# Selective scan: side jobs of TensorE, ScalarE and VectorE moved by one or two places in a 24-place table

## Chip, cores and metric

One core of one Trainium2 chip. The metric is the device time of one execution in microseconds, the median of several runs. The kernel is one launch with a first phase (normalisation, input projection, 3x3 depthwise convolution), a scan phase and a last phase (layer norm, output projection, and a second layer). The change lies in the scan phase alone.

## Reference

Cut to the scan, with b = 8 images, K = 4 directions, 192 channels d, 16 states n, and L = 4096 positions:

```python
xs = stack(x_flat, x_wh, flip(x_flat), flip(x_wh))          # [b, k, 192, L]
x_dbl = einsum('bkdl,kcd->bkcl', xs, x_proj_w)              # 6 + 16 + 16 rows
dts, Bs, Cs = split(x_dbl)
delta = softplus(einsum('bkrl,kdr->bkdl', dts, dt_proj_w) + dt_proj_b)
A = -exp(A_logs)
# for each position:
h = exp(delta * A) * h + (delta * u) * B
y = sum_n(h * C)
# then y + xs * Dk, the four directions put back in place and added
```

The directions k = 1 and k = 3 read the image column by column (transposed).

## Kernel before

**Tiles.** Positions are cut into chunks of 1024, four to a direction: 8 x 4 x 4 = 128 chunks. A chunk is two steps (even, then odd), one for each half of the 192 channels. A step is 12 units: 4 groups g of 4 states by 3 blocks j of 32 channels, so one unit is a tile of 128 partitions (4 states x 32 channels) by 1024 positions. There are 3072 units. Below, e0 to e11 are the units of the even step and o0 to o11 those of the odd step. The program is written by hand for each engine as a loop over units, with semaphores between them; a job that belongs to "place x" stands in the body of the loop at unit x of that engine.

**A unit.** VectorE does the recurrence of a unit in one scan instruction (L739) of decay E and drive. The drive comes in three kinds: DIRECT (14 of 24 units; TensorE spreads B over partitions into PSUM, L597, and VectorE multiplies it by delta*u, L717), DIAGONAL (6 units: e5, e7, e9, o1, o3, o5; TensorE forms the product itself with 32 small matmuls against diagonal copies of B, L639), and POOLED (4 units: e8, e10, o2, o4; GpSimd multiplies, L905). PSUM holds the drives of two units in turn, so TensorE fills unit n+1 only when the scan of unit n-1 has ended. ScalarE makes the decay (L823) and the carry (L829), GpSimd weighs the state with C (L913), TensorE sums over states (L661).

**Side jobs.** Once a chunk or step, these pass through one PSUM tile called stage, one after another; each waits until the last one has been read out (the table `held`, L471 to L482):

- project: the rows dts, B and C of the next chunk, TensorE L581 in two halves of 512 positions; ScalarE copies dts (L763) and then the rest (L764); VectorE splits off a low part (split, L711), which later jobs wait for.
- delta: the second projection, TensorE L591 on 6 partitions; ScalarE applies softplus (L773), with a table load before it and one after it.
- turn_b: B turned onto partitions, TensorE L610, ScalarE L792; from it 32 diagonal copies a chunk (ScalarE L807, numbers in DIAG_EVEN and DIAG_ODD).
- rep: five spreads of C and B, TensorE L597, ScalarE L786 (crep, the four groups of C) and L780 (brep, B for GpSimd), in the order of the list REPS, in which None is brep.
- turn_dlu: delta*u turned, TensorE L620, ScalarE L798.

Before the change, TensorE projects at e9 and e10, ScalarE copies at e11, VectorE splits behind the scan of e11, and TensorE does delta at o1, turn_b at o5, the first rep (brep) at o6, a second delta at o9, and reps at o10, o11, e0, e1. The body of TensorE's loop is in this order:

```python
fill(un + 1)
sum_y(...)
# then the side job of this place
```

Of the kernel before, what the change touches and what calls it, by code (L numbers as in the profile page):

```python
# [308 lines left out]
def scan_phase(nc, ctx, T, S):  # L309
# [5 lines left out]
    ORDER = ((1, 0, 0, 0, 2, 3, 2, 3, 1, 3, 1, 2), (1, 3, 1, 3, 1, 3, 0, 0, 0, 2, 2, 2))  # L315
    KIND = tuple(tuple(DIAGONAL if g == GDIAG else POOLED if g == GPOOL and x in pooled else DIRECT for x, g in enumerate(row))
                 for row, pooled in zip(ORDER, ((8, 10), (2, 4))))
    REPS = (None, 1, 0, 3, 2)
    DIAG_EVEN, DIAG_ODD = {0: 3, 1: 4, 2: 4, 3: 4}, {6: 3, 7: 3, 8: 3, 9: 3, 10: 2, 11: 3}
    wx = T("wx", [C, NK, 2, C + NR])  # L320
    dtw = T("dtw", [C + NR, NK * ND])
    dtb = T("dtb", [C, NK * 2])
# [38 lines left out]
    NCHUNK = NSTEP // 2  # L361
# [37 lines left out]
    def t_of(k, ci):  # L399
        return TC * (ci if k < 2 else NCH - 1 - ci)  # L400
# [20 lines left out]
    def fills(un):  # L421
        return tally(un, DIRECT, DIAGONAL)
# [18 lines left out]
    def loaded(m):  # L441
        return 64 * (m // 2 + 1)
# [27 lines left out]
    order = [("x", 0), ("dt", 0), ("bt", 0), ("lt", 0), ("dt", 1)] + [("rep", 0, i) for i in range(5)]  # L470
    for n in range(NSTEP):  # L471
        c = n // 2 + 1
        if n % 2 == 0:
            order += [("rep", c - 1, i) for i in range(3, 5) if n] + [("lt", n + 1)]
            order += [("x", c)] if c < NCHUNK else []
        elif c < NCHUNK:
            order += [("dt", n + 1), ("bt", c), ("rep", c, 0), ("lt", n + 1), ("dt", n + 2), ("rep", c, 1), ("rep", c, 2)]
    for job, last in zip(order[1:], order):
        if last[0] == "rep":
            held[job] = (rep_out, rep_index(*last[1:]) + 1)  # L480
# [91 lines left out]
    def tensor(e):  # L572
        def project(c, sub):
            b, k, ci, _ = steps[2 * c]
            t0 = t_of(k, ci) + sub * 512
            if sub == 0:
                if ("x", c) in held:
                    e.wait_ge(*held["x", c])
                e.wait_ge(u_in, 32 * (b + 1))
            for h in range(2):  # L580
                r = e.matmul(stage[0:C + NR, sub * 512:(sub + 1) * 512], wx[:, k, h, :], view(k, h, t0, 512),  # L581
                             start=h == 0, stop=h == 1)
            if sub:
                r.then_inc(x_done)
# [16 lines left out]
        def rep(c, i):  # L601
            e.wait_ge(*held["rep", c, i])
            e.wait_ge(sx_split, c + 1)
            spread(stage, c, 2 * GPOOL if REPS[i] is None else 2 * REPS[i] + 1).then_inc(rep_done)

# [72 lines left out]
        for un in range(NUNIT + 12):  # L678
            n, x = divmod(un, 12)
            c = n // 2 + 1  # L680
            fill(un + 1)
            if un >= 5 and (un - 5) % 3 < 2 and (un - 5) // 3 < NG * NSTEP:
                sum_y((un - 5) // 3, (un - 5) % 3)
            if n == NSTEP:
                continue
            if n % 2 == 0:
                if x < 2 and n:
                    rep(c - 1, x + 3)
                if x == 7:
                    turn_dlu(n + 1, 0)  # L690
                    turn_dlu(n + 1, 1)
                if x in (9, 10) and c < NCHUNK:
                    project(c, x - 9)
            elif c < NCHUNK:
                if x == 1:
                    delta(n + 1)
                if x == 5:
                    turn_b(c)
                if x == 6:
                    rep(c, 0)  # L700
                if x in (7, 8):
                    turn_dlu(n + 1, x - 7)
                if x == 9:
                    delta(n + 2)
                if x in (10, 11):
                    rep(c, x - 9)

    def vector(e):
        def split(c):
            e.wait_ge(sx_copied, c + 1)  # L710
            e.tensor_tensor(sx[64:96, c % 2, :], stage[64:96, :], sx[64:96, c % 2, :], ALU.subtract).then_inc(sx_split)  # L711

        def multiply(un):
            m, j = un // 12, un % 3
            e.wait_ge(fill_done, fills(un) + 1)
            e.wait_ge(dur_in[m % 2], loaded(m))
            e.tensor_tensor(P[un % 2], dur[:, slot(m, j), :], P[un % 2], ALU.mult).then_inc(mul_done)  # L717

        def scan(un):
            b, k, ci, half, m, g, j = place(un)  # L720
            cc = cell(un)
            init = 0.0 if ci == 0 else car[:, cc:cc + 1]
            decay, drive = E[:, fills(un) % NE, :], P[un % 2]
            if kind(un) == POOLED:
                e.wait_ge(pool_mul_done, pooled(un) + 1)
                decay, drive = P[un % 2], dbu[:, pooled(un) % NDB, :]
            elif kind(un) == DIRECT:
                e.wait_ge(mul_done, muls(un) + 1)
            else:
                e.wait_ge(fill_done, fills(un) + 1)  # L730
            e.wait_ge(exp_done, un + 1)
            if un >= NH:
                e.wait_ge(hc_done, un - NH + 1)
            if has_carry(un - NH):
                e.wait_ge(carried, carries(un - NH))
            if ci:
                e.wait_ge(carried, carries(un - 24))
            step = 1 if k < 2 else -1
            e.tensor_tensor_scan(H[:, un % NH, ::step], decay[:, ::step], drive[:, ::step], init,  # L739
                                 ALU.mult, ALU.add).then_inc(scan_done)  # L740

        e.wait_ge(consts_in, NCONST)
        e.tensor_copy(selb[:], selbf).then_inc(ve_set)
        e.tensor_reduce(dsum[:], ds[:], AX.X, ALU.add).then_inc(skip_made)
        e.wait_ge(skip_made, 1)
        for half in range(2):
            e.tensor_scalar(dg[:, half, :], idn[0:C, 0:C], dsum[:, half:half + 1], None, ALU.mult).then_inc(skip_made)
        split(0)
        for un in range(NUNIT):
            n, x = divmod(un, 12)  # L750
            c = n // 2 + 1
            if kind(un) == DIRECT:
                multiply(un)
            scan(un)
            if c < NCHUNK and n % 2 == 0 and x == 11:
                split(c)

    def scalar(e):
        def project(c):
            e.wait_ge(x_done, c + 1)  # L760
            if c >= 2:
                e.wait_ge(fill_done, fills(24 * (c - 1)))
            e.copy(dts, stage[C:C + NR, :])  # L763
            e.copy(sx[:, c % 2, :], stage[0:C, :]).then_inc(sx_copied)  # L764
# [10 lines left out]
        def rep(c, i):  # L775
            e.wait_ge(rep_done, rep_index(c, i) + 1)
            if REPS[i] is None:
                if c:
                    e.wait_ge(pool_mul_done, pooled(24 * c))
                e.copy(brep[:], stage).then_inc(rep_out)  # L780
            else:
                if c:
                    e.wait_ge(hc_done, last_of(2 * c - 1, g=REPS[i]) + 1)
                else:
                    e.wait_ge(ve_set, 1)
                e.copy(crep[:, REPS[i], :], stage).then_inc(rep_out)  # L786

# [65 lines left out]
        for un in range(NUNIT + 12):  # L853
            n, x = divmod(un, 12)
            c = n // 2 + 1
            exp(un + 1)
            if has_carry(un - 1):
                carry(un - 1)
            if x == 4 and n:
                copy_y(n - 1)  # L860
            if n == NSTEP:
                continue
            if n % 2 == 0:
                if x < 3 and n:
                    rep(c - 1, x + 2)
                if x in DIAG_EVEN:
                    diagonal(c - 1, sum(DIAG_ODD.values()) + sum(DIAG_EVEN[i] for i in range(x)), DIAG_EVEN[x])
                if x == 8:
                    turn_dlu(n + 1)
                if x == 11 and c < NCHUNK:  # L870
                    project(c)
            elif c < NCHUNK:
                if x == 2:
                    delta(n + 1)
                if x == 6:
                    turn_b(c)
                if x == 7:
                    rep(c, 0)
                if x == 8:
                    turn_dlu(n + 1)  # L880
                if x == 10:
                    delta(n + 2)
                if x == 11:
                    rep(c, 1)
                if x in DIAG_ODD:
                    diagonal(c, sum(DIAG_ODD[i] for i in range(6, x)), DIAG_ODD[x])

    def pool(e):
# [9 lines left out]
        def multiply(un):  # L898
            m, j = un // 12, un % 3
            p = pooled(un)  # L900
            e.wait_ge(dur_in[m % 2], loaded(m))
            e.wait_ge(rep_out, rep_index(m // 2, REPS.index(None)) + 1)
            if p >= NDB:
# [3 lines left out]
        def weigh(un):  # L907
            b, k, ci, half, m, g, j = place(un)
            e.wait_ge(scan_done, un + 1)
            e.wait_ge(rep_out, rep_index(m // 2, REPS.index(g)) + 1)  # L910
            if un >= NHC:
# [811 lines left out]
```

## Time and profile before

| | |
|---|---|
| median of 3 runs | 12463.16 us (12460.2 to 12470.74) |
| profiled execution, its own time | 12428.21 us |
| its span | 12426.3 us |
| TensorE matmuls busy | 10745.4 us, 86% |
| VectorE busy | 10724.7 us, 86% |
| ScalarE busy | 8061.8 us, 65% |
| GpSimd busy | 9752.4 us, 78% |
| first and last split (L711) | 632.8 and 10405.3 us |

The busy shares are averages over three phases. The scan phase is the middle one, and the last scan instruction of it starts at 10514.42 us. Inside it one must go by which instruction of VectorE starts late, and what released it: a timeline row carries this in brackets, [idle us <- releaser]. Matmul ends are modelled, so the start of the next matmul is the better measure of how long TensorE was taken.

### The profile page before, as it was taken

How to read it: one execution, taken by the hardware profiler on the slowest of the kernel's cores; microseconds unless marked ns; L12 is line 12 of the kernel's file. 1: busy time of each engine (PE TensorE's matmuls, PEld its weight loads, DVE VectorE, ACT ScalarE, POOL GpSimd, SP SyncE). 2: the span in 40 equal slices, each digit the busy share in tenths (PEclk: the TensorE clock that was granted, in tenths of full speed). 3: DMA queues.
4: the chain of work that ended last, by engine and by line, in shares of the span. 5: the costliest groups of instructions: out<-in, count | busy, mean ns of one | idle time of the engine just before them, and what ended most of it. 6: DMA issues, size and time to landing. Idle time of an engine off the chain costs nothing. (4 is left out here: it accounts for less than half of the span.)

```text
span 12426.3 us, 236253 instructions
## 1 busy us (share of the span) xinstructions
PE 10745.4 (86%) x91896; PEld 5926.8 (48%) x91896; DVE 10724.7 (86%) x6806; ACT 8061.8 (65%) x13314; POOL 9752.4 (78%) x4238
## 2 busy tenths in 40 slices
PE   8978888888888888888888888888888887799999
PEld 5644444444444444444444444444444443678778
DVE  7789999999999999999999999999999998555554
ACT  3366777677777776777677767776777775444443
POOL 2178999899999999999999989998999998433330
PEclk9977888788878887888788878887888887799999
DMA  3344554455445554555455545544554454221220
GB/s 107 110 111 113 123 133 114 111 123 133 115 112 129 133 116 112 128 132 116 112 129 132 118 109 128 132 113 114 124 130 113 115 123 116 68 62 47 62 62 11
DMA packets 380191, 1363.70 MB, mean 110 GB/s; under 512 B 55270, under 2 KB 55974, under 8 KB 375756
## 3 DMA queue, kind: packets, MB, share of 16 engines
q1 hardware_dynamic: 379084, 1348.57, 46.0%
q8 instruction: 739, 12.11, 0.4%
q14 instruction: 368, 3.01, 0.1%
HBM read 983.45 MB, written 364.90 MB: 109 GB/s over the span
## 5 line engine op out<-in xcount | busy, mean ns | idle before, releaser
L913 POOL TENSOR_TENSOR HC<-H,crep 128x1024 f32<-128x1024 f32 x3072 | 7213.5, 2371 | 836.0 <-DVE H L739 831.4
L739 DVE TENSOR_TENSOR_SCAN H<-E,car,psum 128x1024 f32<-128x1024 f32 x1920 | 4479.2, 2343 | 232.0 <-PE psum L639 174.1
L823 ACT ACTIVATE E<-dlr,am 128x1024 f32<-128x1024 f32 x2560 | 2917.0, 1142 | 68.0 <-DVE H L739 65.6
L597 PE MATMUL psum<-sx,selb 96*128 96x512 f32 x4864 | 2192.0, 560 | 694.9 <-DVE H L739 419.9
L661 PE MATMUL psum<-HC,sely 128*32 128x512 f32 x12288 | 2519.3, 706 | 5.9 <-POOL HC L913 5.1
L639 PE MATMUL psum<-diag,dluT 128*32 128x128 f32 x49152 | 1933.2, 317 | 681.4 <-DVE H L739 676.0
L717 DVE TENSOR_TENSOR psum<-dur,psum 128x1024 f32<-128x1024 f32 x1792 | 2167.9, 1210 | 179.4 <-PE psum L597 175.2
L639 PEld LDWEIGHTS psum<-diag,dluT 128*32 128x32 f32 x49152 | 1624.4, 128 | 1307.2 <-DVE H L739 1176.5
L597 PEld LDWEIGHTS psum<-sx,selb 96*128 96x128 f32 x4864 | 1016.5, 242 | 2141.1 <-DVE H L739 862.5
L739 DVE TENSOR_TENSOR_SCAN H<-E,psum 128x1024 f32<-128x1024 f32 x640 | 1455.1, 2283 | 89.6 <-PE psum L639 68.7
L807 ACT ACTIVATE diag<-idn,blt 128x128 f32<-128x128 f32 x4096 | 1335.4, 394 | 4.1
L823 ACT ACTIVATE psum<-dlr,am 128x1024 f32<-128x1024 f32 x512 | 572.6, 1118 | 1117.9 <-DVE H L739 1116.4
L905 POOL TENSOR_TENSOR dbu<-dur,brep 128x1024 f32<-128x1024 f32 x512 | 1212.6, 2368 | 0.0
L739 DVE TENSOR_TENSOR_SCAN H<-psum,car,dbu 128x1024 f32<-128x1024 f32 x384 | 892.5, 2324 | 0.0
L661 PEld LDWEIGHTS psum<-HC,sely 128*32 128x32 f32 x12288 | 404.3, 119 | 1000.9 <-issue 936.8
L896 POOL TENSOR_TENSOR dlu<-dlt,u 96x1024 f32<-96x1024 f32 x256 | 673.2, 2630 | 133.3 <-ACT dlt L773 133.3
L581 PE MATMUL psum<-u,wx 96*102 96x512 f32 x1024 | 712.6, 824 | 29.1 <-DMA u<-scr_xa 29.1
L829 ACT COPY car<-H 128x1 f32<-128x1 f32 x2304 | 417.5, 181 | 482.8 <-DVE H L739 475.0
L620 PEld LDWEIGHTS psum<-idn,dlu 96*128 96x128 f32 x4096 | 530.9, 206 | 372.3 <-issue 249.0
L620 PE MATMUL psum<-idn,dlu 96*128 96x96 f32 x4096 | 596.6, 298 | 70.9 <-ACT brep L780 70.2
L591 PE MATMUL psum<-dlt,dtw 6*96 6x512 f32 x1024 | 597.4, 709 | 4.3 <-DVE sx L711 3.4
L1568 POOL TENSOR_TENSOR y<-y,tmp 96x1024 f32<-96x1024 f32 x64 | 195.1, 3114 | 458.0 <-DMA tmp<-scr_yk 458.0
(135 smaller groups left out, 11216.4 us busy)
## 6 DMA issues: line engine op xcount, KB each, us to landing
dur<-scr_dlu SPq DMA_DIRECT2D x1024, 384.0 KB, 6.8
dlr<-scr_dl SPq DMA_DIRECT2D x1024, 384.0 KB, 6.8
scr_dl<-dlt SPq DMA_DIRECT2D x256, 384.0 KB, 3.0
scr_dlu<-dlu SPq DMA_DIRECT2D x256, 384.0 KB, 6.8
scr_yk<-yt SPq DMA_DIRECT2D x256, 384.0 KB, 8.3
yp<-scr_yk SPq DMA_DIRECT2D x128, 384.0 KB, 8.8
scr_xa<-xs SPq DMA_DIRECT2D x64, 384.0 KB, 3.5
scr_sz<-xs SPq DMA_DIRECT2D x64, 384.0 KB, 3.4
```

Of the source, the lines that this page charges most:

```text
L581: r = e.matmul(stage[0:C + NR, sub * 512:(sub + 1) * 512], wx[:, k, h, :], view(k, h, t0, 512), start=h == 0, stop=h == 1)
L597: r = e.matmul(o[:, sub * 512:(sub + 1) * 512], selb[:, which, :], sx[:, c % 2, sub * 512:(sub + 1) * 512], start=True, stop=True)
L620: r = e.matmul(stage[:, sub * 512 + k * C:sub * 512 + (k + 1) * C], dlu[:, t0:t0 + 128], idn[0:C, 0:C], start=True, stop=True)
L639: r = e.matmul(P[un % 2][32 * q:32 * q + 32, i * 128:(i + 1) * 128], dluT[:, m % 2, i, 32 * j:32 * j + 32], diag[:, i, q, :], start=True, ...
L661: r = e.matmul(yps[32 * j:32 * j + 32, cols], sely[:], HC[:, (3 * i + j) % NHC, cols], start=g == 0 and k == 1, stop=g == NG - 1)
L717: e.tensor_tensor(P[un % 2], dur[:, slot(m, j), :], P[un % 2], ALU.mult).then_inc(mul_done)
L739: e.tensor_tensor_scan(H[:, un % NH, ::step], decay[:, ::step], drive[:, ::step], init, ALU.mult, ALU.add).then_inc(scan_done)
L807: e.mul(diag[:, i // 4, i % 4, :], idn[:], blt[:, i:i + 1]).then_inc(diag_made)
L823: e.activation(o, dlr[:, slot(m, j), :], ACT.Exp, scale=am[:, ae:ae + 1]).then_inc(exp_done)
L896: e.tensor_tensor(shaped(dlu[:], k), shaped(dl, k), view(k, half, t_of(k, ci), TC), ALU.mult).then_inc(dlu_made)
L905: e.tensor_tensor(dbu[:, p % NDB, :], dur[:, slot(m, j), :], brep[:], ALU.mult).then_inc(pool_mul_done)
L913: e.tensor_tensor(HC[:, un % NHC, :], H[:, un % NH, :], crep[:, g, :], ALU.mult).then_inc(hc_done)
```

## The change

Nothing is computed differently, and no instruction is added or removed. TensorE's projection goes from e9, e10 to e10, e11; ScalarE's copies from e11 to o0; the split from behind the scan of e11 to behind the scan of o0. turn_b goes from o5 (TensorE) and o6 (ScalarE) to o3 and o4. The reps change their order, so that brep is the last instead of the first, and their places: o6, o11, e0, e1, e2 on TensorE; TensorE has no side job at o10 now, and ScalarE no rep at o11. The diagonal copies are 19 in the odd step and 13 in the even one, instead of 17 and 15.

```diff
-    REPS = (None, 1, 0, 3, 2)
-    DIAG_EVEN, DIAG_ODD = {0: 3, 1: 4, 2: 4, 3: 4}, {6: 3, 7: 3, 8: 3, 9: 3, 10: 2, 11: 3}
+    REPS = (1, 0, 3, 2, None)
+    DIAG_EVEN, DIAG_ODD = {0: 3, 1: 3, 2: 3, 3: 4}, {6: 3, 7: 3, 8: 3, 9: 3, 10: 2, 11: 5}
...
 # tensor
-                if x < 2 and n:
-                    rep(c - 1, x + 3)
+                if x < 3 and n:
+                    rep(c - 1, x + 2)
...
-                if x in (9, 10) and c < NCHUNK:
-                    project(c, x - 9)
+                if x in (10, 11) and c < NCHUNK:
+                    project(c, x - 10)
...
-                if x == 5:
+                if x == 3:
                     turn_b(c)
...
-                if x in (10, 11):
-                    rep(c, x - 9)
+                if x == 11:
+                    rep(c, 1)
...
 # vector
-            if c < NCHUNK and n % 2 == 0 and x == 11:
+            if c < NCHUNK and n % 2 == 1 and x == 0:
                 split(c)
...
 # scalar
-                if x < 3 and n:
-                    rep(c - 1, x + 2)
+                if x < 4 and n:
+                    rep(c - 1, x + 1)
...
-                if x == 11 and c < NCHUNK:
+            elif c < NCHUNK:
+                if x == 0:
                     project(c)
-            elif c < NCHUNK:
...
-                if x == 6:
+                if x == 4:
                     turn_b(c)
...
-                if x == 11:
-                    rep(c, 1)
```

TensorE from e8 to o6 of a chunk, before. L581 is the projection, L591 delta, L610 turn_b, L639 a diagonal fill, L597 a direct fill or a rep, L661 a sum:

```order
L661 MATMUL psum<-HC,sely 32x512 x6
L581 MATMUL psum<-u,wx 102x512 x2
L597 MATMUL psum<-sx,selb 128x512 x2
L581 MATMUL psum<-u,wx 102x512 x2
L597 MATMUL psum<-sx,selb 128x512 x2
L661 MATMUL psum<-HC,sely 32x512 x3
L639 MATMUL psum<-diag,dluT 32x128 x32
L661 MATMUL psum<-HC,sely 32x512 x3
L591 MATMUL psum<-dlt,dtw 96x512 x2
L639 MATMUL psum<-diag,dluT 32x128 x32
L661 MATMUL psum<-HC,sely 32x512 x6
L639 MATMUL psum<-diag,dluT 32x128 x32
```

The same stretch with the change:

```order
L661 MATMUL psum<-HC,sely 32x512 x6
L597 MATMUL psum<-sx,selb 128x512 x2
L581 MATMUL psum<-u,wx 102x512 x2
L597 MATMUL psum<-sx,selb 128x512 x2
L661 MATMUL psum<-HC,sely 32x512 x3
L581 MATMUL psum<-u,wx 102x512 x2
L639 MATMUL psum<-diag,dluT 32x128 x32
L661 MATMUL psum<-HC,sely 32x512 x3
L591 MATMUL psum<-dlt,dtw 96x512 x2
L639 MATMUL psum<-diag,dluT 32x128 x32
L661 MATMUL psum<-HC,sely 32x512 x6
L610 MATMUL psum<-selb,sx 128x4 x8
```

The first fill (that of e11) is now ahead of both halves of the projection, the second half stands behind the fill of o0 and a sum, and turn_b stands ahead of the diagonal fill of o5.

VectorE around the split, before, and then with the change (the listing calls the scan SCALAR_TENSOR_TENSOR):

```order
L739 SCALAR_TENSOR_TENSOR H<-psum,car,dbu 128x1024
L717 TENSOR_TENSOR psum<-dur,psum 128x1024
L739 SCALAR_TENSOR_TENSOR H<-E,car,psum 128x1024
L711 TENSOR_TENSOR sx<-psum,sx 32x1024
L717 TENSOR_TENSOR psum<-dur,psum 128x1024
L739 SCALAR_TENSOR_TENSOR H<-E,car,psum 128x1024 x2
```

```order
L739 SCALAR_TENSOR_TENSOR H<-psum,dbu 128x1024
L717 TENSOR_TENSOR psum<-dur,psum 128x1024
L739 SCALAR_TENSOR_TENSOR H<-E,psum 128x1024
L717 TENSOR_TENSOR psum<-dur,psum 128x1024
L739 SCALAR_TENSOR_TENSOR H<-E,psum 128x1024
L711 TENSOR_TENSOR sx<-psum,sx 32x1024
L739 SCALAR_TENSOR_TENSOR H<-E,psum 128x1024
```

The split has passed one multiply and one scan (those of o0); the scan of o1 now comes right behind it. (The second listing is of a chunk without carries, at the start of a direction, which is why `car` is missing.)

## Rows read from the trace of the kernel before

**Rows 1.** Page, part 1: busy time of each engine.
```profile
PE 10745.4 (86%) x91896; PEld 5926.8 (48%) x91896; DVE 10724.7 (86%) x6806; ACT 8061.8 (65%) x13314; POOL 9752.4 (78%) x4238
```
**Rows 2.** The split's line: durations in ns, first and last start in us.
```profile
L711 DVE TENSOR_TENSOR sx<-psum,sx x128: 1222/1222/1224, 632.8 to 10405.3; 32x1024 fp32r<-32x1024 f32 x128
```
**Rows 3.** Waits, 1500 to 10500 us, 116 chunks: us in total, times, longest.
```profile
DVE H L739 <- PE psum L639: 223.7, 238, 1.6
...
PEld psum L597 <- ACT dlt L773: 214.9, 117, 2.9
...
DVE psum L717 <- PE psum L597: 134.0, 112, 2.4
DVE sx L711 <- ACT sx L764: 113.6, 61, 1.9
```
**Rows 4.** VectorE's timeline, e10 to o5, next direction odd: start, us, idle before.
```profile
4162.16 2.33 DVE L739 TENSOR_TENSOR_SCAN H<-psum,car,dbu 128x1024 f32<-128x1024 f32 x1
4165.63 1.23 DVE L717 TENSOR_TENSOR psum<-dur,psum 128x1024 f32<-128x1024 f32 x1 [1.14 <-PE psum L597]
...
4171.11 1.22 DVE L711 TENSOR_TENSOR sx<-psum,sx 32x1024 fp32r<-32x1024 f32 x1 [1.87 <-ACT sx L764]
...
4173.63 4.58 DVE L739 TENSOR_TENSOR_SCAN H<-E,car,psum 128x1024 f32<-128x1024 f32 x2
...
4181.98 2.35 DVE L739 TENSOR_TENSOR_SCAN H<-E,car,psum 128x1024 f32<-128x1024 f32 x1 [1.52 <-PE psum L639]
...
4186.48 2.32 DVE L739 TENSOR_TENSOR_SCAN H<-E,car,psum 128x1024 f32<-128x1024 f32 x1
```
**Rows 5.** TensorE's timeline in the same chunk, e9 to o6.
```profile
4161.47 3.66 PE L581 MATMUL psum<-u,wx 96*102 96x512 f32 x4
...
4165.43 3.59 PE L581 MATMUL psum<-u,wx 96*102 96x512 f32 x4
...
4172.04 1.03 PE L661 MATMUL psum<-HC,sely 128*32 128x512 f32 x6
4173.01 1.95 PE L591 MATMUL psum<-dlt,dtw 6*96 6x512 f32 x4
4178.27 3.64 PE L639 MATMUL psum<-diag,dluT 128*32 128x128 f32 x64 [3.31 <-DVE H L739]
4181.68 2.55 PE L661 MATMUL psum<-HC,sely 128*32 128x512 f32 x12
4184.38 1.95 PE L639 MATMUL psum<-diag,dluT 128*32 128x128 f32 x64
4186.62 0.73 PE L597 MATMUL psum<-sx,selb 96*128 96x512 f32 x2 [0.29 <-DVE H L739]
...
4189.13 1.05 PE L610 MATMUL psum<-selb,sx 96*128 96x4 f32 x8
```
**Rows 6.** ScalarE's timeline in the same chunk, e11 to o2.
```profile
4169.06 1.00 ACT L763 COPY dlt<-psum 6x1024 f32<-6x1024 f32 x1 [4.34 <-PE psum L581]
...
4180.88 1.28 ACT L823 ACT_TABLE_LOAD   x1
4182.17 1.12 ACT L823 ACTIVATE psum<-dlr,am 128x1024 f32<-128x1024 f32 x1
```
**Rows 7.** Windows of that chunk: PE, PEld, DVE, ACT, POOL busy, PEclk, DMA share, GB/s.
```profile
4173.00:4178.20 5.20, 1.96 (x7) 0.56 (x4) 5.16 (x4) 2.13 (x3) 3.32 (x2) 0.81 0.00 0
4178.20:4181.90 3.70, 3.63 (x67) 3.35 (x70) 2.25 (x2) 3.65 (x5) 3.70 (x3) 0.50 0.06 19
```
**Rows 8.** TensorE's second projection half where the next direction is even.
```profile
5087.13 1.88 PE L581 MATMUL psum<-u,wx 96*102 96x512 f32 x4
```
**Rows 9.** VectorE's split in that chunk.
```profile
5091.42 1.22 DVE L711 TENSOR_TENSOR sx<-psum,sx 32x1024 fp32r<-32x1024 f32 x1
```
**Rows 10.** Timeline of the softplus at o10: TensorE behind it, and VectorE.
```profile
5051.90 2.08 PE L597 MATMUL psum<-sx,selb 96*128 96x512 f32 x4 [2.45 <-ACT dlt L773]
5051.94 1.21 DVE L717 TENSOR_TENSOR psum<-dur,psum 128x1024 f32<-128x1024 f32 x1
```

More of the change, by code:

```diff
@@ L473, in scan_phase @@
         if n % 2 == 0:
-            order += [("rep", c - 1, i) for i in range(3, 5) if n] + [("lt", n + 1)]
+            order += [("rep", c - 1, i) for i in range(2, 5) if n] + [("lt", n + 1)]
             order += [("x", c)] if c < NCHUNK else []
         elif c < NCHUNK:
-            order += [("dt", n + 1), ("bt", c), ("rep", c, 0), ("lt", n + 1), ("dt", n + 2), ("rep", c, 1), ("rep", c, 2)]
+            order += [("dt", n + 1), ("bt", c), ("rep", c, 0), ("lt", n + 1), ("dt", n + 2), ("rep", c, 1)]
     for job, last in zip(order[1:], order):
```

## Prediction

> **What bounds the kernel.** I read the busy shares first: TensorE and VectorE are both at 86%, GpSimd at 78% [rows 1]. These are averages over three phases, so I took the scan phase by itself. The split occurs 128 times, from 632.8 to 10405.3 us [rows 2], which is 9772.5 / 127 = 76.9 us a chunk. VectorE's own work in a chunk is 24 scans of 2.25 us (two back to back take 4.58 us, and overlap their neighbours by 0.09), 14 multiplies of 1.25 us and a split of 1.25 us, 72.8 us in all [rows 4]. So VectorE sets the pace, and some 4 us a chunk are its waits. The waits over 116 chunks say for what: 223.7 us for diagonal fills (1.9 a chunk), 134.0 us for direct fills (1.2 a chunk), and 113.6 us for ScalarE's copy ahead of the split, in only 61 of 116 chunks, so 1.86 us each time it occurs [rows 3]. What the change does to these three is the whole question. TensorE also waits 117 times for the softplus, 214.9 us [rows 3]; that is the wait which the free place at o10 takes away.
>
> **1. Projection from e9, e10 to e10, e11, the split behind o0.** Half of the chunks are followed by a chunk of an odd direction, whose projection reads the image by columns. There a half takes 3.59 to 3.66 us [rows 5]; for an even direction it takes 1.88 us [rows 8], and the split then follows the scan of e11 (5089.05 + 2.35) without a gap [rows 9]. In the slow chunk VectorE stands 1.14 us at the multiply of e11 and 1.87 us at the split [rows 4], 3.01 us in all.
>
> With the change the fill of e11 is ahead of both halves, so the 1.14 us go. The split I walk through in that chunk. The scan of e9 ends at about 4162.25; a direct fill takes 0.6 to 0.7 us, so the first half starts at 4162.9. A half and a fill behind it take 4165.43 - 4161.47 = 3.96 us, so the sum starts at 4166.9; it holds TensorE for 4173.01 - 4172.04 = 0.97 us; the second half starts at 4167.8 [rows 5]. From there to ScalarE's first copy it is 4169.06 - 4165.43 = 3.63 us, and from that to the split 2.05 us [rows 4 to 6]: the split can start at 4173.5. VectorE wants it when the scan of o0 ends. The scan of e11 would end at 4169.24 - 1.14 = 4168.1, multiply and scan of o0 take 3.5 us, so at 4171.6. A stall of 1.9 us is left, of 3.01. The gain is 1.1 us in 64 chunks, **-70 us**. It is not the whole 3 us, because the second half moves behind a fill and a sum as the split moves behind a unit. In the other 64 chunks there was no stall, and with a half of 1.88 us there is none after: 0.
>
> **2. The diagonal fill of o3.** It starts when the scan of o1 ends and takes 3.64 us at 1.2 GHz, against 1.95 us for the same work at 2.4 GHz [rows 5]. VectorE has one scan of 2.25 us to cover it, and stands 1.52 us [rows 4]. The granted clock was 0.81 over the 5.2 us before it, in which TensorE worked 1.96 us, and 0.50 during it [rows 7]. Delta (L591) now waits for the later split, so it moves from just behind the sum to just behind the split, into that pause. It is 1.95 us of work on 6 partitions in the same stretch, and I take it that the clock still falls in most chunks. In the 64 slow chunks the pause between the sum before it and the fill is shorter, since projection and diagonal fill end later: before, from 4173.0 to 4178.3, 5.3 us; now the second half from 4167.8 holds TensorE to 4170.4, the fill to 4172.3, the sum to 4173.3, and the scan of o1 ends at 4173.5 + 1.25 + 2.3 = 4177.1, so 3.8 us. I give half of these fills the higher clock or part of it. ScalarE then sets the limit: its decay for o4 ends at 4183.29 [rows 6], and the scan of o4, which starts at 4184.24, could be 0.9 us earlier and no more. Half of 0.9 or so, 0.5 us x 64 = **-32 us**. The bounds are 0 and 0.9 x 64 = -58.
>
> By the Trainium skill, "ScalarE: Activation LUTs", section "What ACT_TABLE_LOAD costs", a switch of tables is a load of about 1283 ns and a drain of about 1380 ns, 2.66 us together. The load is 1.28 us here too, but the next activation starts 0.01 us behind it [rows 6], so this trace has no such drain. With two drains the decay of o4 would be 2.8 us later than it is, this term would be 0, and the place left free behind the softplus would be worth more than I give it.
>
> **3. Delta itself at the lower clock.** Where the clock falls while delta runs in its new place, it ends late and pushes the fill of o3. Bounds: 0, and 0.9 us, twice delta's 1.95 less what lies before the scan of o1 ends (2.3 + 0.7 of slack in the walk above). I take 0.1 us in the 63 chunks that have no shorter pause: **+6 us**.
>
> **4. turn_b from o5 to o3.** It takes 0.9 to 1.05 us of TensorE [rows 5] and now stands between the sums and the diagonal fill of o5. In the trace the sums start at 4181.68, last 2.55 us, and the fill of o5 starts at 4184.38 as the scan of o3 ends; it ends at 4186.33, and the scan of o5 starts at 4186.48 [rows 4, 5]. So the slack is 0.15 us of fill and some 0.15 to 0.5 us before it. Bounds: 0.1 us (sums at the higher clock) and 1.0 us (all at the lower). I take 0.3 us in the 63 even chunks and 0.2 in the others, whose sums run faster more often: 19 + 13 = **+32 us**. It waits for the softplus of o2 as well, which has ended when the table load behind it starts at 4180.88, 0.8 us before the sums [rows 5, 6]: covered.
>
> **5. What I cost at nothing.** The rep that leaves o10: TensorE stood 2.45 us for the softplus, but it had already filled the next unit, and VectorE's multiply went on at 5051.94 [rows 10]; the cover is one filled unit of 3.5 us, and it is there with or without the change. The rep added at e2 lies in a place of 3.5 us that holds a fill, a sum and a spread, 0.6 + 1.0 + 0.6; at the lower clock at most twice that, 4.4 us, 0.9 too much for once, which the fill's lead of a whole unit less its own time takes. brep is copied at e3, and GpSimd needs it only behind its weighing of e3. crep for group 1 now waits at o7 on GpSimd's weighing of o4; ScalarE loses some tenths there, and the decay of the next unit is already made; were this cover gone, it would be a tenth or two a chunk. The diagonal copies: two more at o11 where a copy of 1.0 us has gone, 0.35 us less over e1 and e2, four behind brep at e3, done just before the fill of e5. The DMA queue's order is untouched; its transfers hang on dl_made and dlu_made, whose places stay.
>
> **Sum.** -70 - 32 + 6 + 32 = -64 us. The profiled execution took 12428.2 us and would take 12364. The median of the three runs is 35 us above the profiled one, and I put the change on the median: 12463.2 - 64 = **12399 us**. A measurement of this kernel can tell about 0.2%, 25 us, from no change.
>
> **Rivals.**
>
> *A second stall takes the first's place (slower).* The price is in terms 3 and 4 at their upper bounds: turn_b's 1.0 less 0.15 of slack, and 0.4 of delta, 1.3 us in all 127 chunks, +165 us, less the 70 of term 1: 12558 us. It turns slower from 0.55 us a chunk on. For it: the fill of o5 has hardly slack, and TensorE is at the lower clock when the sums begin. Against it: the fill of o5 took 1.95 us, so the clock is back by then. Chance 0.18.
>
> *The pause is filled and the clock stays up.* If delta in the pause keeps the clock at 2.4 GHz, the fill of o3 takes 1.95 us in all chunks, and ScalarE's limit leaves 0.9 us of gain: 0.92 x 127 = 117 us, terms 3 and 4 fall away, -187: 12276 us. The clock over the stretch was 0.81 although delta ran in it [rows 7], which speaks against it. The Trainium skill, "TensorE: Matmul & The Clock Gate", says that the clock is throttled by default and that activity releases it, which speaks for it. Chance 0.12.
>
> *The change does not do what it says.* The split's stall comes back in full, because the sum ahead of the second half, or that half at the lower clock, makes it 1.1 us later than in my walk. Then only terms 2 to 4 are left: 12469 us. The walk has no slack on TensorE, but all of it lay at the full clock. Chance 0.20.
>
> **How the numbers follow.** My forecast has 0.50, with a range of its own from 12360 to 12440. Faster by over 0.2% (below 12438): 0.46 of it, the second rival, and 0.02 of the third: 0.60. Slower (above 12488): 0.15 of the first rival and 0.03 of the third: 0.18. Within: 0.22. The range leaves out the second rival's centre and the upper half of the first, and reaches from 12330 to 12500.
>
> **What would show it.** L717 waits for L597 fall from 134 us to about 60 (those at o11 stay), L711 waits stay at about 60 in number and near 1.9 us each. A scan at o5 with a wait of 0.1 to 0.5 us is new. The wait at o3 stays near 1.5 us where the next direction is even, and is under 1 us in half of the others. TensorE no longer waits for the softplus, and nothing comes of it. I am wrong if the split's stall is gone or over 2.5 us, if the wait at o5 is over 0.7 us, or if the clock no longer falls at o1 to o3.

## Result and profile after

| | before | changed |
|---|---|---|
| median | 12460.2 us (5 runs) | 12542.27 us (5 runs, 12530.65 to 12545.39) |
| span of the profiled execution | 12426.3 us | 12541.4 us |
| ratio, 95% interval | | 1.0074 [1.0053, 1.0094] |
| TensorE matmuls busy | 10745.4 us | 10963.0 us |
| VectorE busy | 10724.7 us | 10726.0 us |
| ScalarE, GpSimd busy | 8061.8, 9752.4 us | 8063.9, 9759.2 us |

The changed kernel is slower by 0.74%. I had forecast 0.5% faster, with an upper end of 12500 us. VectorE does the same work as before [rows 1], so what was added is time in which it waits. TensorE's busy time rose by 218 us for the same matmuls. (In the experiments below, each ratio is taken to the kernel before as timed together with that experiment; its median lay between 12435 and 12462 us.)

The waits of VectorE in the changed kernel, over the same stretch as [rows 3] (us in total, times, longest):

```profile
DVE H L739 <- PE psum L639: 249.5, 224, 2.7
DVE psum L717 <- PE psum L597: 191.7, 87, 2.4
DVE sx L711 <- ACT sx L764: 129.8, 59, 3.4
```

All three rose: diagonal fills by 26 us, direct fills by 58, the split by 16. The direct fills surprise: the change took away their wait at e11. I therefore added up VectorE's gaps by place, in both traces, over chunks 8 to 125 (worked out from the starts and ends of its instructions, in us a chunk; the last two columns belong to experiments below):

| place | before | changed | turn_b back | two matmuls added |
|---|---|---|---|---|
| multiply of e11 | 0.60 | 0 | 0 | 0 |
| split | 0.95 | 1.10 | 1.18 | 1.29 |
| scan of o3 | 1.38 | 1.47 | 1.31 | 1.16 |
| scans of o4, o5 | 0.01 | 0.36 | 0.07 | 0.48 |
| multiply of o11 | 0.47 | 1.64 | 0.55 | under 0.05 |
| all others | 0.65 | 0.47 | 0.42 | 0.31 |
| sum | 4.06 | 5.04 | 3.53 | 3.24 |

Changed less before is 0.98 us, times 127 chunks 124 us; the spans differ by 115. The loss is the multiply of o11, 1.17 us a chunk or 149 us. Nothing was moved there except that a rep went away behind it.

**What happens at o11.** The timeline of VectorE in the changed kernel, in a chunk of direction 3, at o10 and o11:

```profile
4317.46 2.35 DVE L739 TENSOR_TENSOR_SCAN H<-E,car,psum 128x1024 f32<-128x1024 f32 x1
4321.99 1.23 DVE L717 TENSOR_TENSOR psum<-dur,psum 128x1024 f32<-128x1024 f32 x1 [2.19 <-PE psum L597]
```

In the same chunk of the kernel before, the two follow each other without a gap:

```profile
4284.02 2.35 DVE L739 TENSOR_TENSOR_SCAN H<-E,car,psum 128x1024 f32<-128x1024 f32 x1
4286.29 1.21 DVE L717 TENSOR_TENSOR psum<-dur,psum 128x1024 f32<-128x1024 f32 x1
```

The fill that the multiply waits for stands behind the delta of o9. TensorE in the changed kernel, from o7 on:

```profile
4307.04 1.13 PE L620 MATMUL psum<-idn,dlu 96*128 96x96 f32 x8 [0.47 <-ACT crep L786]
4309.35 1.22 PE L597 MATMUL psum<-sx,selb 96*128 96x512 f32 x2 [1.17 <-DVE H L739]
4310.50 1.93 PE L661 MATMUL psum<-HC,sely 128*32 128x512 f32 x6
4312.36 2.02 PE L620 MATMUL psum<-idn,dlu 96*128 96x96 f32 x8
4314.09 1.20 PE L597 MATMUL psum<-sx,selb 96*128 96x512 f32 x2
4315.22 1.93 PE L661 MATMUL psum<-HC,sely 128*32 128x512 f32 x6
4317.08 3.72 PE L591 MATMUL psum<-dlt,dtw 6*96 6x512 f32 x4
4320.73 2.08 PE L597 MATMUL psum<-sx,selb 96*128 96x512 f32 x4
```

And before:

```profile
4274.41 1.13 PE L620 MATMUL psum<-idn,dlu 96*128 96x96 f32 x8 [0.63 <-ACT brep L780]
4275.91 0.74 PE L597 MATMUL psum<-sx,selb 96*128 96x512 f32 x2 [0.36 <-DVE H L739]
4276.58 1.06 PE L661 MATMUL psum<-HC,sely 128*32 128x512 f32 x6
...
4281.07 2.85 PE L591 MATMUL psum<-dlt,dtw 6*96 6x512 f32 x4
4283.85 1.22 PE L597 MATMUL psum<-sx,selb 96*128 96x512 f32 x2
```

The order of TensorE's work from o7 up to the fill of o11 is the same in both. In the changed kernel each group takes up to twice as long from the second fill on (1.22 for 0.74, 1.93 for 1.06, 3.72 for 2.85), until the fill of o11 comes 3.3 us behind the start of the scan of o10 (4320.73 and 4317.46), where before it came 0.2 us ahead of it (4283.85 and 4284.02). The windows say why. Their borders are starts of scans: the rows of before are o7, o8 and o9, those of the changed kernel o5 and o6 together, o7, o8, o9, and o10. The columns are those of [rows 7]; PEclk stands behind POOL. Before:

```profile
4273.55:4277.05 3.50, 2.50 (x17) 1.42 (x16) 3.46 (x3) 2.82 (x6) 3.50 (x2) 1.00 0.33 130
4277.05:4280.56 3.51, 2.79 (x22) 1.42 (x16) 3.48 (x3) 1.83 (x5) 3.51 (x3) 1.00 0.72 161
4280.56:4284.07 3.51, 3.51 (x11) 0.90 (x6) 3.47 (x3) 3.49 (x8) 3.11 (x2) 0.70 1.04 212
```

Changed:

```profile
4299.93:4306.94 7.01, 6.50 (x24) 2.14 (x24) 6.95 (x5) 4.85 (x11) 7.01 (x4) 1.00 1.04 221
4306.94:4310.44 3.50, 2.23 (x10) 1.47 (x10) 3.47 (x2) 2.17 (x6) 3.50 (x2) 0.70 0.39 157
4310.44:4313.95 3.51, 3.51 (x14) 1.79 (x14) 3.47 (x2) 0.00 (x0) 3.50 (x3) 0.50 1.02 196
4313.95:4317.45 3.50, 3.50 (x12) 1.19 (x11) 3.47 (x2) 3.03 (x8) 2.37 (x2) 0.50 1.04 211
4317.45:4323.25 5.80, 5.80 (x11) 1.93 (x13) 3.58 (x2) 5.45 (x10) 4.65 (x3) 0.50 0.49 117
```

The stretch from a start of a scan to the fall itself, first in the kernel before (from o8) and then in the changed one (from o6), and the stretch behind the fall in the changed kernel:

```profile
4277.05:4281.99 4.94, 4.22 (x24) 1.81 (x19) 4.91 (x3) 3.26 (x8) 4.94 (x3) 1.00 0.81 174
4303.43:4308.34 4.91, 4.21 (x20) 1.72 (x18) 4.86 (x3) 3.53 (x7) 4.91 (x4) 1.00 0.99 266
4308.34:4310.44 2.10, 1.09 (x2) 0.50 (x2) 2.08 (x2) 0.77 (x2) 2.10 (x1) 0.50 0.03 12
```

The granted clock falls to 1.2 GHz in the place of o7, two places earlier than before, and stays there through o10. It falls at 4308.34, so the pause of 1.17 us, from about 4308.2 to 4309.35, lies nearly all behind the fall and follows it rather than explains it. Ahead of the fall stands only the pause of 0.47 us, and TensorE was at work for 4.21 of the last 4.91 us, as much as ahead of the later fall in the kernel before (4.22 of 4.94 us). What did change is where the work lies: the last matmuls of o6 ended at 4306.6, 0.4 us before the scan of o7 began, where before they ended 0.2 us after it had begun (4273.8 and 4273.55), since the eight of turn_b had gone from o5. This one chunk does not show why the clock falls; that is what the experiments are for. Over chunks 8 to 125, the clock is at 1.2 GHz in 38% of the time of o8 before and in 97% in the changed kernel (54% and 87% for o9). And the delta decides: in the changed kernel 88 of these 118 chunks wait over 0.3 us at o11, and in all 88 the delta of o9 took 3.72 us; in the 30 others it took 2.08 us or less. Before it was 32 chunks, again all with 3.72 us.

### The profile page after: what moved, and what is told of

The parts are those of the page before. It is cut to its first block and busy times, and to the rows that moved or that the text cites. A ratio compares the mean times of both kernels' runs of the same rounds, so it can differ in the third digit from the quotient of the medians.

```text
span 12541.4 us, 236253 instructions
## 1 busy us (share of the span) xinstructions
PE 10963.0 (87%) x91896; PEld 5828.1 (46%) x91896; DVE 10726.0 (86%) x6806; ACT 8063.9 (64%) x13314; POOL 9759.2 (78%) x4238
## 5 line engine op out<-in xcount | busy, mean ns | idle before, releaser
L597 PE MATMUL psum<-sx,selb 96*128 96x512 f32 x4864 | 2164.4, 553 | 920.9 <-DVE H L739 569.9
L661 PE MATMUL psum<-HC,sely 128*32 128x512 f32 x12288 | 2665.9, 744 | 6.3 <-POOL HC L911 5.3
L717 DVE TENSOR_TENSOR psum<-dur,psum 128x1024 f32<-128x1024 f32 x1792 | 2163.9, 1208 | 239.9 <-PE psum L597 239.9
L597 PEld LDWEIGHTS psum<-sx,selb 96*128 96x128 f32 x4864 | 990.0, 243 | 2514.4 <-DVE H L739 1256.3
L639 PE MATMUL psum<-diag,dluT 128*32 128x128 f32 x49152 | 1721.4, 297 | 194.2 <-DVE H L739 167.0
L639 PEld LDWEIGHTS psum<-diag,dluT 128*32 128x32 f32 x49152 | 1471.7, 120 | 780.5 <-DVE H L739 628.5
L661 PEld LDWEIGHTS psum<-HC,sely 128*32 128x32 f32 x12288 | 411.9, 122 | 1030.9 <-issue 864.4
L591 PE MATMUL psum<-dlt,dtw 6*96 6x512 f32 x1024 | 724.0, 842 | 163.0 <-DVE sx L711 162.1
L620 PEld LDWEIGHTS psum<-idn,dlu 96*128 96x128 f32 x4096 | 585.2, 224 | 441.2 <-issue 318.4
L581 PE MATMUL psum<-u,wx 96*102 96x512 f32 x1024 | 712.6, 824 | 29.4 <-DMA u<-scr_xa 29.4
L620 PE MATMUL psum<-idn,dlu 96*128 96x96 f32 x4096 | 656.9, 318 | 67.5 <-ACT crep L786 66.6
L798 ACT COPY dluT<-psum 128x768 f32<-128x768 f32 x256 | 204.4, 799 | 673.2 <-PE psum L620 672.9
```

Source lines behind the costliest of these rows:

```text
L591: r = e.matmul(stage[0:C, sub * 512:(sub + 1) * 512], dtw[C:C + NR, k * ND + half * C:k * ND + (half + 1) * C], dts[:, sub * 512:(sub + 1) ...
L597: r = e.matmul(o[:, sub * 512:(sub + 1) * 512], selb[:, which, :], sx[:, c % 2, sub * 512:(sub + 1) * 512], start=True, stop=True)
L620: r = e.matmul(stage[:, sub * 512 + k * C:sub * 512 + (k + 1) * C], dlu[:, t0:t0 + 128], idn[0:C, 0:C], start=True, stop=True)
L639: r = e.matmul(P[un % 2][32 * q:32 * q + 32, i * 128:(i + 1) * 128], dluT[:, m % 2, i, 32 * j:32 * j + 32], diag[:, i, q, :], start=True, ...
L661: r = e.matmul(yps[32 * j:32 * j + 32, cols], sely[:], HC[:, (3 * i + j) % NHC, cols], start=g == 0 and k == 1, stop=g == NG - 1)
```

## Experiments

Three theories for the earlier fall of the clock. **Theory 1**: turn_b gone from o5 leaves TensorE too little to do from o5 to o7. **Theory 2**: with the new order of reps, ScalarE's copy of crep at o7 waits for GpSimd's weighing of o4, and TensorE's turn_dlu waits for that copy. **Theory 3**: the later projection and split shift the rest.

**turn_b back.** The changed kernel with

```diff
-                if x == 3:
+                if x == 5:        # tensor
                     turn_b(c)
-                if x == 4:
+                if x == 6:        # scalar
                     turn_b(c)
```

> The changed kernel with turn_b back at o5 on TensorE and o6 on ScalarE; all else as changed. Theory 1 (turn_b gone from o5 leaves TensorE pauses at o5 to o7, the clock falls by o8, and the delta of o9 takes 3.7 us and holds up the fill of o11): the waits of L717 for L597 fall from 192 us to about 60 (0.5 us a chunk), the new wait at o5 goes (0.34 us a chunk), and the kernel takes about 12400 us, 0.4% to 0.6% under the kernel before. Theory 2 (the rep order: crep at o7 waits for GpSimd and delays turn_dlu): the waits of L717 stay near 190 us, only the 0.34 us go, about 12500 us.

Measured: 12352.8 us, ratio to the kernel before 0.9918 [0.9902, 0.9934]. Its waits:

```profile
DVE H L739 <- PE psum L639: 195.3, 176, 2.4
DVE sx L711 <- ACT sx L764: 141.8, 60, 3.6
DVE psum L717 <- PE psum L597: 65.0, 31, 2.4
```

So this one job of about 1 us of TensorE, moved by two places, is worth 1.6% of the kernel: it turns 0.7% slower into 0.8% faster. L717's waits are 65 us, where theory 1 said about 60. The time is some 50 us below what I expected.

**turn_b moved alone.** The same two lines changed from 5 to 3 and from 6 to 4 in the kernel before.

> The kernel before with turn_b alone moved, to o3 on TensorE and o4 on ScalarE. Theory 1: the clock falls by o8 in nearly all chunks, the wait at the multiply of o11 rises from 0.5 to about 1.6 us a chunk and o5 gets its 0.3 us: +1.4 us x 127 = +180 us, 1.4% slower than before. Theory 2: o5 alone, +40 us, 0.3% slower.

Measured: 12554.99 us, ratio 1.0084 [1.0068, 1.0101].

```profile
DVE H L739 <- PE psum L639: 251.4, 275, 1.6
DVE psum L717 <- PE psum L597: 184.1, 177, 2.4
DVE sx L711 <- ACT sx L764: 111.9, 60, 1.9
```

By itself it makes the kernel 0.84% slower, which is as much as the whole loss, but it is not the same loss. By place, o5 waits 0.65 us a chunk (before nothing), and o11 0.82 (before 0.47). So here most of the price is paid where turn_b arrives, some 80 us, and only some 45 us at o11. Theory 1 had expected 1.6 us at o11 and a kernel 1.4% slower, and was half right: the clock is low in 90% of o8 as it said, but at o9 in 58%, not 87%, and the delta of o9 took 3.72 us in 44 of the 118 chunks, not in 88. I can't say why from these runs.

**Projection and split moved alone**, in the kernel before: the parts of the diff for `project` and `split`, nothing else.

> The kernel before with only the projection moved to e10 and e11, ScalarE's copies to o0, and the split behind the scan of o0. Theory 1: L717 loses the waits of e11 (134 to about 60 us), the split keeps about 2 us in half of the chunks, nothing changes from o5 on: 0.4 us a chunk faster, -50 us, 0.4%. Theory 3 (the later split itself, with delta in the pause, brings the low clock at o8): L717 near 190 us and a time at or above the kernel before.

Measured: 12385.9 us, ratio 0.995 [0.9933, 0.9966]; L717's waits are 96 us. The moved projection brings 0.5%, a little more than the 0.4% forecast here, so theory 3 falls as the cause of the loss. It is not quite nothing, though: of L717's waits only 60 us were to be left. The wait at o11 rose from 0.47 to 0.77 us a chunk, and the delta of o9 took 3.72 us in 47 chunks instead of 32. The two moves do not add up: turn_b alone brings 0.35 us a chunk at o11, the projection alone 0.30, the whole change 1.17.

**The list of reps in its old order**, in the changed kernel:

```diff
-    REPS = (1, 0, 3, 2, None)
+    REPS = (None, 1, 0, 3, 2)
```

> The changed kernel with the list of reps in its old order, brep first at o6 and the four of C behind it, the places as changed. ScalarE's copy at o7 is then of brep and does not wait for GpSimd's weighing of o4. Theory 1: no difference from the changed kernel, 12520 to 12560 us, L717 waits near 190 us. Theory 2: turn_dlu comes on time, L717 waits fall to about 60 us and the time to about 12400 us. Group 1 of C is now copied at e0, just before it is needed: GpSimd may wait for ScalarE there, at no cost to VectorE.

Measured: 12527.78 us, ratio 1.0059 [1.0044, 1.0074], L717's waits 188.6 us. That is the changed kernel to within its interval. Theory 2 falls.

**A stand-in at o5.** The changed kernel, turn_b still at o3, and its eight matmuls once more at o5:

```diff
+        def stand_in(c):
+            e.wait_ge(bt_copied, c + 1)
+            for k in range(NBLK):
+                e.matmul(stage[:, 4 * k:4 * k + 4], sx[:, c % 2, k * 128:(k + 1) * 128],
+                         selb[:, 2 * GDIAG, 0:128:32], start=True, stop=True)
...
+                if x == 5:
+                    stand_in(c)
```

> The changed kernel, turn_b still at o3, and at o5 the same eight matmuls once more, into the same columns, which nobody reads. This tells whether it is TensorE's missing work at o5 that lowers the clock at o8, or something that follows from turn_b being earlier. Theory 1 (missing work): the clock holds as in the kernel before, L717 waits fall from 192 to about 65 us, the wait at o5 stays at 0.34 us a chunk, about 12400 us. Rival (the earlier turn_b does it through ScalarE's order or GpSimd): 12540 us, L717 waits stay near 190 us.

Measured: 12465.43 us, ratio 1.0031 [1.002, 1.0042]; the waits of its multiply, which is L725 in this kernel, are 112.5 us:

```profile
DVE psum L725 <- PE psum L597: 112.5, 52, 2.4
```

Work that serves nothing wins back 0.4% of the time, and by place 0.7 of the 1.1 us a chunk at o11. Theory 1 had said about 12400 us and 65 us of waits, its rival 12540 us and 190 us; the measurement lies between the two, nearer to theory 1. The clock is low in 64% of o8, against 54% with turn_b itself there, so it comes back in part, not in full.

**Two matmuls added at o6 and o7.** If the loss is the clock, a kernel with more work must be faster. The changed kernel with

```diff
+        def keep(n):
+            for i in range(n):
+                e.matmul(yps[96:128, i * 512:(i + 1) * 512], sely[:], crep[:, 2, i * 512:(i + 1) * 512],
+                         start=True, stop=True)
...
+                if x in (6, 7):
+                    keep(1)
```

> The changed kernel with one matmul of 512 columns at o6 and one at o7, each about 0.9 us of TensorE, whose result nobody reads; turn_b stays at o3. If the loss is the clock from o7 to o9, more work on TensorE makes the kernel faster: the waits at o11 fall from 1.64 to about 0.4 us a chunk, -1.2 x 127 = -150 us, about 12390 us. If the loss is something else (what turn_b or the rep order does to ScalarE and GpSimd), the added work changes nothing or costs up to 0.3 us a chunk: 12540 to 12580 us.

Measured: 12305.15 us, ratio 0.9879 [0.9855, 0.9904]. The changed kernel stood at 1.0074, so 1.9% come from adding two matmuls of 512 columns a chunk, 254 in all, to the program. The multiply (L723 in this kernel) no longer waits for a direct fill in any chunk of the scan phase. That is 85 us better than the forecast of 12390 us: I had left 0.4 us a chunk at o11, and there is none, and o3 waits 0.3 us less as well. TensorE at o7, and at the delta of o9:

```profile
4226.93 1.05 PE L616 MATMUL psum<-crep,sely 128*32 128x512 f32 x2
4227.96 1.13 PE L624 MATMUL psum<-idn,dlu 96*128 96x96 f32 x8
4229.77 0.74 PE L597 MATMUL psum<-sx,selb 96*128 96x512 f32 x2 [0.67 <-DVE H L745]
...
4234.93 1.95 PE L591 MATMUL psum<-dlt,dtw 6*96 6x512 f32 x4
4236.81 0.73 PE L597 MATMUL psum<-sx,selb 96*128 96x512 f32 x2
```

and its windows of o7, o8 and o9:

```profile
4227.40:4230.90 3.50, 2.83 (x17) 1.42 (x16) 3.46 (x3) 2.54 (x6) 3.50 (x2) 1.00 0.77 254
4230.90:4234.41 3.51, 2.79 (x21) 1.42 (x16) 3.48 (x3) 1.81 (x5) 3.51 (x3) 1.00 0.73 154
4234.41:4237.91 3.50, 3.14 (x12) 0.85 (x6) 3.46 (x3) 3.48 (x8) 2.81 (x2) 1.00 1.06 218
```

The added matmul (L616) fills the pause at o7, the clock is 1.00 to the end of o9, delta takes 1.95 us, and the fill behind it is done in time. This shows that the loss at o11 was the clock: nothing but TensorE's work was added, and the wait went with the low clock (0% of o8, where the changed kernel has 97%).

**The rep back at o10.** The changed kernel with `rep(c, 1)` at o10 on TensorE and o11 on ScalarE, so that the place behind the softplus isn't free.

> The changed kernel with the second rep back at o10 on TensorE (o11 on ScalarE), so the place behind the softplus is not free; order of the reps and the rest as changed. The prediction costed that place at nothing: then 12530 to 12555 us, no change of L717 waits (190 us). If the free place was worth TensorE's 2.5 us of waiting: up to 1 us a chunk slower, 12650 us. If leaving it free is part of what lowered the clock: faster, 12480 us or less.

Measured: 12544.55 us, ratio 1.0064 [1.0046, 1.0081]; L717's waits 191.3 us. In this kernel TensorE waits for the softplus 116 times:

```profile
PEld psum L597 <- ACT dlt L773: 157.3, 116, 3.7
```

and it costs nothing, as term 5 had it.

**A better version.** turn_b back at o5, the second projection half ahead of the sum at e11, and ScalarE's copies swapped, so that the split waits for one of them only:

```diff
-            e.copy(dts, stage[C:C + NR, :])
-            e.copy(sx[:, c % 2, :], stage[0:C, :]).then_inc(sx_copied)
+            e.copy(sx[:, c % 2, :], stage[0:C, :]).then_inc(sx_copied)
+            e.copy(dts, stage[C:C + NR, :]).then_inc(dts_copied)
```

> The changed kernel with turn_b back at o5 and o6, the second projection half ahead of the sum at e11 instead of behind it, and ScalarE's two copies swapped, so that the split waits for the first of them (1.0 us earlier). If the split's wait is the chain half, copy, copy, as in the prediction's walk: 0.97 + 1.0 us go of 2.1 to 2.4 in half of the chunks, L711 waits fall from 142 us to under 30, about 1.0 us x 127 = -110 us against the version with turn_b back alone: 12240 us. If another wait takes its place (the fill of o1, or the fill of o3 at the low clock): 12300 us or more.

Measured: 12249.59 us, ratio 0.9854 [0.9836, 0.9872]. The split no longer waits; a wait of 0.35 us a chunk for the fill of o1 takes a part of its place.

**The pause at o0 filled**, with two of the matmuls above (`keep(2)` at o0, ahead of delta), on top of that:

> As the one before, and in the pause at o0, ahead of delta, two matmuls of 512 columns whose result nobody reads (32 partitions of a PSUM tile that are not used). If work in the pause holds the clock: the fill of o3 takes 1.95 us, its wait falls from 1.3 us a chunk to about 0.3, limited by ScalarE's decay of o4 to a gain of 0.9 us: about -90 us against the one before. If the pause ahead of delta has no say, since the clock falls for what follows: the same time, or up to 0.3 us a chunk slower for the 1.7 us of added work.

Measured: 12196.69 us, ratio 0.9812 [0.9794, 0.9829]. The clock at o2 is low in 31% of the time instead of 56%, and o3 and o4 together wait 0.84 us a chunk instead of 1.05. The direction is right, the size 53 us of the 90 that I had said: the fill of o3 still takes over 2.1 us in 41 of the 118 chunks (59 before this step).

**And one matmul each at o6 and o7**, on top:

> As the one before, and one such matmul each at o6 and o7. If TensorE's work from o5 to o8 holds the clock until the delta of o9: the wait at the multiply of o11 (0.5 us a chunk) goes, -60 us. If the added 0.85 us each push the fills of o7 and o8 late: up to +0.5 us a chunk slower.

Measured: 12173.86 us, ratio 0.9792 [0.9775, 0.981], the fastest of all, but its interval overlaps the one before. The forecast of -60 us missed. The clock at o8 is low in 15% of the time instead of 49%, and yet o11 waits 0.32 us instead of 0.34. What counts for o11 is the clock during the delta of o9: at o9 it is low in 25% of the time instead of 31%, and that delta still takes 3.72 us in 15 chunks (20 before this step). A high clock at o8 alone does not win the wait.

## Why the prediction was wrong

**Term 1, projection and split: right.** Forecast: the 1.14 us of e11 go, the split waits 1.9 us where the next direction is odd, -70 us. Measured: 0.60 us a chunk at e11 are gone and the split has 0.15 more, -57 us. In the chunk of [rows 4] the wait is now 2.10 us. VectorE's timeline of the changed kernel there:

```profile
4209.61 1.22 DVE L711 TENSOR_TENSOR sx<-psum,sx 32x1024 fp32r<-32x1024 f32 x1 [2.10 <-ACT sx L764]
```

TensorE's:

```profile
4203.86 3.66 PE L581 MATMUL psum<-u,wx 96*102 96x512 f32 x4
4207.45 1.95 PE L639 MATMUL psum<-diag,dluT 128*32 128x128 f32 x64
```

And ScalarE's:

```profile
4207.55 1.01 ACT L763 COPY dlt<-psum 6x1024 f32<-6x1024 f32 x1 [3.32 <-PE psum L581]
4208.57 1.01 ACT L764 CAST sx<-psum 96x1024 fp32r<-96x1024 f32 x1
```

The half at 4203.86, a copy 3.69 us later and the split 2.06 us behind that: the chain of the walk, some 0.2 us longer. With the half ahead of the sum and the copies swapped the wait was gone, as the chain has it.

**Terms 2 and 3, the fill of o3: too favourable.** Forecast -32 and +6 us. By place and kind of chunk, o3 waits 1.22 us instead of 1.44 where the next direction is odd, and 1.73 instead of 1.32 where it is even: -14 and +26 us. The second is delta at the lower clock, whose bound of 0.9 us I had named and of which I took 0.1. My walk also has a slip: it lets the second half hold TensorE from 4167.8 to 4170.4, 2.6 us, where [rows 5] have 3.59, and so the pause it gives, 3.8 us, is about a microsecond too long. Measured in that chunk it is 3.0 us (the sum ends at 4210.25, the fill starts at 4213.27), and the fill still took 3.35 us. ScalarE's limit at o4 was there: five of the six chunks that wait at o4 had a fill of o3 of 1.95 us.

**Term 4, turn_b in front of the fill of o5: about right in size.** Forecast +32 us. Measured 0.35 us a chunk at o4 and o5, +44 us. How it is divided between the chunks is not as forecast: o5 waits 0.59 us where the next direction is even and 0.10 where it is odd (I had 0.3 and 0.2). And with turn_b moved alone o5 waits 0.65 us, +82 us, so the size holds only together with the later projection.

**The step that failed is term 5**, what I cost at nothing, and with it the one-sided reading of term 4. I priced turn_b where it arrives and gave the place that it leaves no price at all. It left TensorE with less to do from o5 to o7; the clock fell at o7 instead of o8 or later; the fills, sums, turn_dlu and above all the delta of o9 ran at 1.2 GHz; and the multiply of o11 waited. That is 149 us, 138 of which go again when turn_b is put back (1.64 to 0.55 us a chunk). Without the 149 the gaps would sum to -25 us, the forecast's sign though not its -64; with turn_b back the kernel is 0.8% faster. I had read the granted clock only around o3, where VectorE waits. The rows for it were there: in the trace of before o11 waited 0.47 us a chunk already, in 32 of 118 chunks, each time behind a delta of 3.72 us. A wait that occurs in some chunks and not in others is a place that stands near an edge. None of my three signs of being wrong could catch this, since they all look at e11 to o5: the split's stall was 2.2 us each time, the wait at o5 0.34 us, and the clock still fell at o1 to o3. Only the forecast for L717, about 60 us where 191.7 came, pointed to o11.

**The first rival** gave 12558 us, near the measured time, but by another mechanism. Its waits at o5 were to be 0.85 us and are 0.36. The measured time is no confirmation of it, and its deciding point (0.55 us a chunk at o3 and o5) was not reached. **The second rival** did not occur: with delta moved into the pause the clock is low in 88% of o2, against 92% before. Its idea was tested with the filled pause: two matmuls more there brought o2 from 56% to 31%. Whether it matters that delta's matmuls have only 6 partitions, no run shows. The Trainium skill, "TensorE: Matmul & The Clock Gate", section "What's actually happening", says that activity releases the clock. The added matmuls agree with that, in the pause and at o6 and o7. **The third rival**, that the stall before the split comes back in full, did not occur.

What stays open: what exactly in TensorE's work sets the moment at which the clock falls; why turn_b alone slows the o9 delta in fewer chunks than the full change does; and why its stand-in wins back 0.7 us of 1.1 and not all.

## What to carry to other kernels

A job that is moved has two prices: what it delays where it arrives, and what its absence does where it leaves. On TensorE the second can be larger, since less work between two waits can cost the clock for a long stretch behind it (in the chunk shown it was at 1.2 GHz for 17 us, from 4308.34 to 4325.40); before moving a side job, look at the granted clock of the places behind the one it leaves. Where a wait appears in some periods of a loop only, find what differs between them before calling the place unchanged.

## What I had not expected of the hardware

- Work that nobody reads made this kernel faster: two matmuls a chunk, some 2 us of TensorE in 76 to 78, brought 12542 to 12305 us.
- In the chunk shown the clock fell although TensorE had not stood still for more than 0.47 us in the 8 us before: it was at work for 6.50 of the 7.01 us of o5 and o6, and for 1.13 of the 1.40 us of o7 before the fall.
- Neither TensorE's busy time nor its mean clock over the whole execution tells which kernel is faster. For the same matmuls the busy time is 10745 us before and 10963 in the changed kernel, but 10748 with turn_b moved alone, which is just as slow, and 10851 with the projection moved alone, which is faster than before. The mean granted clock is 0.851 before and 0.852 changed: the changed kernel has it lower at o7 to o9 and higher at other places (at e0 it is low in 20% of the time instead of 80%). What counts is the clock under the fill that VectorE waits for.
